# Graph attention with residual and layer norm on one core: third tile's masks ahead of the second table, x by rows a quad at a time, an early flag, set-up waits reordered

## The reference

```python
def _L0_gnn_ref(inlayer, adj_mat, W, w1, b1, w2, b2):
    in_fts = W @ inlayer.T
    f1 = (w1 @ in_fts).T + b1
    f2 = (w2 @ in_fts).T + b2
    logits = f1 + f2.T
    bias_mat = jnp.where(adj_mat > 0, 0.0, NEG_INF).astype(logits.dtype)
    coefs = jax.nn.softmax(jax.nn.leaky_relu(logits) + bias_mat, axis=-1)
    vals = coefs @ inlayer
    return vals
x = _layernorm(x + _L0_gnn_ref(x, adj, ...), axis=-1)
```

## Time and profile before

| what | us |
|---|---|
| time, median of 3 runs (273.82 to 276.17) | 274.12 |
| the profiled execution | 275.19 |
| its span, first to last instruction | 273.5 |
| PE busy | 258.2 |
| DVE busy | 242.6 |
| ACT busy | 195.6 |
| POOL busy | 67.2 |

### The profile page before, as it was taken

The page is one execution under the profiler, slowest core; times in us unless marked ns, Lnnn a source line. Parts: engine busy times, 40 slices in busy tenths (PEclk is TensorE's granted clock), DMA queues, the critical chain, the costliest instruction groups (busy, mean ns, idle before and its releaser), DMA issues.

```text
span 273.5 us, 5997 instructions
## 1 busy us (share of the span) xinstructions
PE 258.2 (94%) x2195; PEld 225.6 (82%) x2195; DVE 242.6 (89%) x309; ACT 195.6 (72%) x296; POOL 67.2 (25%) x98
## 2 busy tenths in 40 slices
PE   2999988799999999999999999999999999999991
PEld 2989877688888888888888888888888888888880
DVE  2888999988888899999999999999998999999963
ACT  2479999949999996999199919991999198003140
POOL 4002046930000006300630063006300630054150
PEclk9999999999999999999999999999999999999998
DMA  6999999999999999999999999999999999801011
GB/s 196 256 298 309 311 313 282 285 272 311 313 315 318 315 314 315 323 339 315 316 324 342 318 316 280 361 328 327 240 335 309 309 285 337 226 2 38 0 49 31
DMA packets 22562, 73.64 MB, mean 269 GB/s; under 512 B 3090, under 2 KB 4244, under 8 KB 22548
## 3 DMA queue, kind: packets, MB, share of 16 engines
q1 hardware_dynamic: 11184, 35.17, 42.9%
q10 hardware_dynamic: 9956, 34.64, 42.0%
q0 software_dynamic: 1408, 3.67, 4.7%
HBM read 71.37 MB, written 2.10 MB: 269 GB/s over the span
## 4 chain that ended last, share of the span: by engine, by line
DVE 58%; PE 16%; issue 8%; ACT 7%; DMA 7%; DVEq 1%; ACTq 1%; POOL 1%; POOLq 0%
DVE mn L743 19%; PE ps L1091 16%; DVE msk L756 11%; DVE mn L748 11%; DMA nat<-in_adj 5%; DVE post L855 3%; ACT sgn L474 3%; DVE ybt L870 2%; DVE bns L875 2%; ACT bt L542 2%; DVE ntot L860 2%; DVE post L857 2%; ACT post L518 2%; DMA msk<-in_x 2%; DVE mv L879 1%
## 5 line engine op out<-in xcount | busy, mean ns | idle before, releaser
L1091 PE MATMUL ps<-bt,msk 128*128 128x258 f16 x2048 | 232.1, 274 | 3.6 <-DVE msk L756 2.7
L1091 PEld LDWEIGHTS ps<-bt,msk 128*128 128x128 fp8e5 x2048 | 200.5, 98 | 34.2 <-issue 4.6
L474 ACT ACTIVATE sgn<-f2b,nf1l 128x1024 int8<-128x1024 f32 x128 | 136.4, 1144 | 5.2 <-POOL flag L409 4.0
L743 DVE TENSOR_SCALAR mn<-nat 128x4096 int8<-128x4096 int32 x32 | 73.1, 2284 | 5.0 <-DMA nat<-in_adj 4.6
L416 POOL TENSOR_SCALAR nmr<-mv 128x4 f32<-128x4 f32 x7 | 12.8, 1835 | 143.5 <-DVE mv L879 143.5
L756 DVE STREAM_TRANSPOSE msk<-mn 128x1024 uint32<-128x1024 uint32 x32 | 39.8, 1245 | 2.6
L748 DVE SCALAR_TENSOR_TENSOR mn<-sgn,mn 128x1024 uint32<-128x1024 uint32 x32 | 39.2, 1225 | 3.0 <-ACT sgn L474 2.0
L623 ACT ACTIVATE ybt<-ybt,nmr,rstd 128x128 f32<-128x128 f32 x28 | 11.5, 483 | 38.7 <-POOL nmr L421 38.7
L616 ACT ACTIVATE post<-ps,ac 128x258 f32<-128x258 f32 x60 | 24.8, 467 | 10.9 <-PE ps L1091 10.9
L761 DVE TENSOR_SCALAR msk<-msk 128x1024 uint32<-128x1024 uint32 x32 | 22.2, 695 | 1.0
L427 POOL DMA_DIRECT2D out<-ybt x24 | 13.7, 572 | 16.3 <-ACT ybt L623 14.9
(11 more groups left out here) (115 smaller groups left out, 105.2 us busy)
## 6 DMA issues: line engine op xcount, KB each, us to landing
nat<-in_adj SPq DMA_DIRECT2D x64, 512.0 KB, 15.1
nat<-in_adj ACTq DMA_DIRECT2D x64, 512.0 KB, 17.6
xn<-in_x POOLq DMA_DIRECT2D x4, 512.0 KB, 19.8
out<-ybt POOLq DMA_DIRECT2D x24, 64.0 KB, 6.6
msk<-in_x SPq DMA_DIRECT2D x8, 128.0 KB, 4.2
msk<-in_x ACTq DMA_DIRECT2D x8, 128.0 KB, 4.5
out<-ybt SPq DMA_DIRECT2D x4, 64.0 KB, 1.8
out<-post SPq DMA_DIRECT2D x4, 32.0 KB, 2.4
```

The costliest lines, as they stand in the source:

```text
L474: ins = act.activation(sgn[:, c, g * JA:(g + 1) * JA], f2b[:, :], ACT.Sign, bias=nf1l[:, bass.ds(G * t + g, 1)], scale=-1.0)
L743: dve.tensor_scalar(mn[:, c % 2], nat[:, c], 0, EDGE, ALU.is_gt, ALU.mult).then_inc(cast_done, 1)
L1091: ins = pe.matmul(ps[:, 2 * c + m, 0:2 * DV], mask_f[c][m][:, n // KB, n % KB, :], btv[m][:, n, :], start=(n == 0), stop=(n == NK - 1))
```

## The change

It does the following, and nothing else:

- **DVE, tile 2.** `cast`, `combine` and `turn` of tile 2 now stand in the middle of table 0's work, right behind the first chunk's `scale_x`. Table 0's chunks are made in the order 1, 0, 2, 3 (`ORDER`), ACT scales chunk 0 alone (`scale_act`), DVE the other three. ACT's `signs` of tile 2 stand ahead of all of table 0's `split_x`, and those of tile 3 have two `split_x` in between.
- **PE.** The minus sums of tile 2 stand ahead of all plus sums, and the plus sums of tiles 0, 1 and 2 are interleaved by chunk. In tile 0's minus sums all four `gram` stand behind the first chunk.
- **Table 1.** DVE scales chunk 3 for its larger part, and ACT only four blocks instead of eight. All `scale_x` stand ahead of the first cast, and `low_x` of chunks 2 and 3 behind the second `spread_f1`.
- **x by rows.** `xn` comes a quad at a time: quads 0 and 1 (eight transfers of 64 KB) where the four transfers of 512 KB were, and each later quad in POOL's loop ahead of a store. The loop is written out instead of being a loop in registers.
- **Flag.** Three of POOL's range tests stand ahead of the loads of `xn`, and the rest are four instructions instead of ten.
- **Set-up.** Only one block's f2 comes from PE, and two blocks' from ACT by sums. The bias product b1 + b2 comes ahead of `f1_columns`; the first `spread_f1` stands behind the fourth product of f2 on DVE, ahead of its sum; the copy of the first `nf1l` is ACT's and stands ahead of `xT_out(2)`; `xT_out(4)` and `xT_out(5)` come later than the fifth and sixth did, among `signs` and `split_x`.

```diff
@@ POOL @@
+            def load_rows(q, s):
+                for g in range(G):
+                    pool.dma_start(xn[g * SQ:(g + 1) * SQ, QT * q:QT * (q + 1), :],
+                                   x_g[g][:, QT * q:QT * (q + 1)]).then_inc(xn_in[s], 16)
+            pool.wait_ge(gst_ready, 1)
+            pool.tensor_tensor(rng[:, 0:1], gst[:, 0:1], gst[:, 1:2], ALU.add).then_inc(rng_step, 1)
...
             pool.wait_ge(f1_made, 2)
             pool.wait_ge(cast_done, 2)
-            for g in range(G):
-                pool.dma_start(xn[g * SQ:(g + 1) * SQ, :, :], x_g[g]).then_inc(xn_in, 16)
+            load_rows(0, 0)
+            load_rows(1, 1)
...
-                with pool.Fori(1, NQ // 2) as turn:
+                for turn in range(1, NQ // 2):
+                    load_rows(2 * turn, 0)
                     store(2 * turn - 2, 0)
                     rows(2 * turn - 1, 1)
+                    load_rows(2 * turn + 1, 1)
                     store(2 * turn - 1, 1)
                     rows(2 * turn, 0)
@@ ACT @@
             xT_out(1)
-            load_far(1, 1)
-            xT_out(2)
...
+            act.wait_ge(nf1_made, 1)
+            act.activation(nf1l[:, 0:FIRST * KB], ps[:, 6, 384:384 + FIRST * KB], ACT.Copy).then_inc(nf1l_ready, 1)
+            xT_out(2)
...
-            xT_out(4)
-            signs(0, 0, between=lambda: xT_out(5))
+            signs(0, 0, between={1: lambda: xT_out(4)})
             load_far(3, 3)
             split_x(1, 0)
-            xT_out(6)
+            xT_out(5)
+            split_x(1, 1)
...
             rows_out()
+            act.wait_ge(nf1l_ready, 2)
+            signs(2, 2)
+            act.wait_ge(cast_done, 2)
+            load_far(QT + 1, 1)
+            split_x(0, 1)
             scale_act(0)
             split_x(0, 0)
...
-            signs(3, 3, between=next_tile)
+            signs(3, 3, between={1: lambda: split_x(0, 2), 2: lambda: split_x(0, 3)})
@@ DVE @@
             dve.wait_ge(cs_ready[0], 1)
+            scale_x(0, 1)
+            stat_max(1, 2, 4)
+            cast(2, 2, 0)
+            stat_out(1, 2, 4)
+            combine(2, 2)
+            dve.wait_ge(y_ready[0], 1)
+            turn(2, 2)
+            plus(0, 0)
+            low_x(0, 1)
+            plus(1, 1)
             scale_x(0, 2)
-            stat_max(1, 2, 4)
+            low_x(0, 0)
             scale_x(0, 3)
-            plus(0, 0)
-            low_x(0, 0)
-            plus(1, 1)
-            stat_out(1, 2, 4)
-            low_x(0, 1)
+            dve.wait_ge(y_act, 1)
+            plus(2, 2)
             low_x(0, 2)
             low_x(0, 3)
-            cast(2, 2, 0)
-            combine(2, 2)
-            dve.wait_ge(y_act, 2)
-            turn(2, 2)
-            plus(2, 2)
             cast(3, 3, 0)
@@ PE @@
-            for h in range(BCH):
-                plus_sums(h, range(2))
             pe.wait_ge(xT_ready, NB)
             pe.wait_ge(turn_done, 3)
             edge_sums(2, 1)
-            for h in range(BCH):
-                plus_sums(h, [2])
+            pe.wait_ge(den_ready[0], 1)
+            pe.wait_ge(xeps_ready, 1)
+            plus_sums(ORDER[0], range(2))
+            plus_sums(ORDER[1], range(2))
+            plus_sums(ORDER[0], [2])
+            plus_sums(ORDER[1], [2])
+            plus_sums(ORDER[2], range(3))
+            plus_sums(ORDER[3], range(3))
```

More of the change, by code:

```diff
@@ L447, in _ @@
             with pool.Else():
+                for q in range(2, NQ):
+                    load_rows(q, q % 2)
                 with pool.Fori(0, NT) as t:
@@ L469, in load_far, with signs @@
                     load_part(act, t, c, a)
-            def signs(t, c, between=None):
+            def signs(t, c, between={}):
                 for g in range(G):
@@ L520, in scale_act, with scale_first @@
                 ins.then_inc(y_act, 1)
+            def scale_first():
+                act.wait_ge(cs_ready[1], 1)
+                for i in range(KB):
+                    n = (BCH - 1) * CN + i
+                    ins = act.activation(ybuf[:, BCH - 1, i], xl_chunk(BCH - 1)[:, i], ACT.Copy, scale=cs[:, 1, n:n + 1])
+                ins.then_inc(y1_act, 1)
             def rows_out():
@@ L801, in _ @@
             turn(0, 0)
-            scale_x(1, 2)
             low_x(1, 1)
-            low_x(1, 2)
             spread_f1(1, FIRST * KB, NK, 7, 0)
@@ L977, in _ @@
                 dve.wait_ge(g_f2_ready, 2 * A)
-                dve.wait_ge(xn_in, 16 * G)
+                for i in range(2):
+                    dve.wait_ge(xn_in[i], 8 * G * NQ)
                 STEPS = 7
@@ L1154, in _ @@
             edge_sums(3, 1)
-            for h in range(BCH):
+            for h in ORDER:
                 plus_sums(h, [3])
```

200 lines of the change are left out of this document (93 added, 107 removed).

## The result

| what | before | changed |
|---|---|---|
| median of twelve runs, us | 274.64 | 276.52 |
| lowest to highest | 273.59 to 276.52 | 275.80 to 278.08 |
| the profiled execution | 275.19 | 275.80 |
| its span | 273.5 | 273.6 |
| time outside the span, median | 1.7 | 2.1 |

The ratio of the times is 1.0074, with a 95% interval of 1.0052 to 1.0097. The changed kernel is 2 us slower. I had forecast 273.5 and a range up to 275.8. By the bound of 1% this is the case to which I gave 0.82, but the sign was wrong, and the range too short by 0.7 us. Of the 3.0 us between forecast and median, 0.5 is the base: I had started from the median of three runs of the kernel before, 274.12, and twelve give 274.64.

What follows compares the result with a forecast made beforehand. PE was taken to bound the kernel: time before tile 2, 215 us of products, 6.1 us of tail. The 0.6 us gain ahead of tile 4 gave 274.6 like the profiled run, median 273.5, range 271.8 to 275.8.

Steps and rivals of the forecast that it cites:

- the case to which I gave 0.82: Whole kernel: time the same within 1% (2.7 us), between 271.4 and 276.9 us; chance 0.82.
- What bounds the kernel: Whole kernel: time before tile 2, plus PE's unbroken 215 us of products, plus 6.1 us behind the last.
- my 51 to 54: POOL's flag: ready at 51 to 54 us, DVE wants it at 58.6; its coming earlier is worth 0.
- The written-out loop on POOL: 0 ... The tail is unchanged.: POOL's loop and the end: writing the loop out costs 0, as POOL mostly waits; the tail stays as it was.
- Cost on the path 0: x by rows, a quad at a time in the loop: costs 0; without tile 10's cover at most 0.9 us per quad.
- The new waits: PE's set-up: 1.1 us of waiting for `xT_out(2)`, and 0 to 0.5 for `xT_out(5)`.
- the gain of 0.6 us: PE up to tile 4's first product: 66.1 us instead of 66.75, the whole gain of the change.
- the 44 that I had named as a sign of being wrong: PE's unbroken row: prediction wrong if it starts before 44 us with DVE ready earlier than forecast.
- my 44.6: PE at tile 2: minus sums can start at 44.6 us (30.5 plus DVE's 14.1), against 52.42.
- DVE was the bound after all: Rival: DVE bounds the kernel, relief from 4.6 us of waits for `adj` counts with the 0.6; 269 us, chance 0.07.
- The clock falls: Rival: PE's clock drops in 2.4 us of idle ahead of tile 2, costing 1.6 us; 275.1 us, chance 0.08.
- POOL is held up at its loads: Rival: POOL's x issues cost over about 1.7 us each, flag late; at 3 us each 283 us, chance 0.03.

Runs made afterwards that it cites:

- e2: The kernel before with POOL's loop over quads written out and nothing else; 274.23 us, ratio 0.9992.
- e5: The kernel before with 28 more loads of 512 bytes each on POOL's queue, loop still in registers; 276.11 us, ratio 1.0036.
- e6: The changed kernel with a drain in each of POOL's three turns; 276.15 us, ratio 1.0035.
- e12: The changed kernel with x by rows in one go (4 issues of 512 KB) and drains in POOL's turns; 274.30 us, ratio 0.9968.
- e16: e6 with 14 products nobody uses ahead of PE's wait for tile 2's masks; 275.34 us, ratio 1.0025.
- e9: The changed kernel with each load of x for quads 2 to 7 bringing 2 KB instead of 64 KB, still 58 issues; 276.72 us, ratio 1.0060.
- e3: The kernel before with x by rows a quad at a time on POOL's queue and the loop written out; 276.83 us, ratio 1.0084.
- e1: The changed kernel with x by rows again in four transfers of 512 KB on POOL's queue; 274.70 us, ratio 1.0029.
- e13: e9 with 14 products nobody uses ahead of PE's wait for tile 2's masks; 276.30 us, ratio 1.0063.
- e14: The changed kernel with 14 products nobody uses ahead of PE's wait for tile 2's masks; 276.21 us, ratio 1.0071.
- e7: The changed kernel with drains in POOL's turns and the last quad's stores issued a tile at a time; 275.12 us, ratio 1.0028.
- e8: The kernel before with drains in POOL's turns and the last quad's stores issued a tile at a time; 274.60 us, ratio 0.9987.
- e11: The kernel before with x by rows in three parts, drains in POOL's turns and the loop written out; 275.91 us, ratio 1.0043.
- e10: The changed kernel with x by rows in three parts (38 issues) and drains in POOL's turns; 275.15 us, ratio 1.0007.
- e15: e12 with POOL's loop in registers and 14 products nobody uses ahead of PE's wait for tile 2's masks; 274.80 us, ratio 1.0015.
- e4: The changed kernel with x by rows (32 transfers of 64 KB) on SP's queue and POOL's loop in registers; 296.75 us, ratio 1.0819.

## Why the prediction was wrong

**What bounds the kernel: right up to the last product.** PE never waited behind tile 2, DVE's waits for `adj` and ACT's for the flag were hidden from PE, and the flag brought nothing. POOL had it ready at 55.9, later than my 51 to 54, and DVE came to it at 57.8. What failed is the step from PE's end to the program's. I had read "6.1 us behind the last product" as DVE's chain behind PE. It was two chains, and POOL's drain ended within half a microsecond of SP's, out of sight of all rows I had quoted.

**"The written-out loop on POOL: 0 ... The tail is unchanged."** This is the first step that failed: the tail was 7.9 us instead of 6.1. I had priced each new issue by its time on POOL (0.81 us, hidden) and by its bytes (hidden), not by what it leaves for the end. The written-out loop is innocent (e2); the 28 issues in it aren't: by themselves they make 2.3 us of drain, and 1.0 us of time by the ratio or 1.5 by the medians (e5).

**x by rows: "Cost on the path 0".** This is the second. For PE it held in the profiled execution. But DVE's position at the end counts too, and the 2.14 us that it had in hand stood in the earlier trace rows, which I used for another purpose. In the changed kernel's timeline a tile costs DVE 5.54 us (from the cast at 241.85 to the next at 247.39) and a quad's moments 5.6 (from 252.96): 27.8 us of the 28.7 that PE takes for a quad. So DVE gains at most 0.9 us a quad on PE, and it gains that in the kernel before as well, where it is just as full (27.9 us from the cast at 158.28 to the one at 186.17). What it loses against the kernel before by a wait, 1.4 us at 146 us and 0.2 for tile 29 at 230.6, it doesn't get back by the end: it came out 1.4 us later against PE. Nor did its waits for `adj` shrink, as I had forecast: 4.8 us instead of 4.6. By e6 and e12, which have the short drain, this costs up to 1.85 us; by e16 it is 0.5 to 1.0.

**The sum of the two.** The end is the later of two chains, and each of my two steps lengthens one of them. In us behind the last product, from the traces:

| kernel | DVE's idle time ahead of the last join | SP at its drain | POOL's drain ends | span ends |
|---|---|---|---|---|
| before | 2.14 | 5.8 | 5.4 | 6.1 |
| e5 (issues alone) | 2.33 | 5.9 | 7.7 | 7.9 |
| e6 (x in the loop, short drain) | 0.24 | 6.6 | 2.9 | 6.9 |
| changed | 0.70 | 6.9 | 7.6 | 7.9 |
| e9 (issues, little of x) | 2.78 | 5.8 | 7.6 | 7.9 |
| e3 | none | 7.9 | 8.7 | 8.9 |
| e12 (neither) | 2.77 | 5.8 | 2.9 | 6.1 |

In the changed kernel's trace POOL's drain alone sets the tail, and DVE's lateness costs nothing beside it: with DVE in time (e9) the tail is the same. With the drain short (e6) the lateness is what is left, 0.8 us of tail. Where DVE has no time in hand at all (e3), POOL's chain is late as well, and both count. In executions without a profile the shares are not known. By the medians e5 and e6 cost 1.5 us each and the two together 1.9 to 2.2 (changed, e3); by the ratios it is 1.0 each and 2.0 to 2.3, so the times alone don't show whether the two add.

**Outside the span** I had counted no change, and it is 0.4 us. It seems to go with the transfers written down in POOL's program rather than with those that run: 1.7 in the kernel before and in e5 (58 run, most of them in a loop), 1.8 in e1, e2 and e12, 2.0 in e3, 2.1 in the changed kernel, e9, e13 and e14. That isn't shown: in e6, e7 and e16, which have the same transfers and the drains, single executions have either 1.8 to 1.9 or 2.2 to 2.4 us.

**From the start to tile 2: the steps came as forecast, but the gain didn't.** The new waits were 0.84 and 0.48 us (I had 1.1, and 0 to 0.5). DVE's chain from the second `spread_f1` (29.50) to PE's start on tile 2 (43.62) took 14.1 us, as summed, and PE's idle time was 1.6 to 2.3 (2.4). But the first mask product came later against the first work on x than I had it. Before, 22.9 us lie between them (29.30 - 6.38, and the same in e2, e3 and e5; 23.3 and 23.5 in e8 and e11); in the twelve traces with the new set-up it is 24.0 (changed, e10, e14, e16) to 25.5 (e7). On the mean the loss is 1.5 us instead of 1.1 (24.53 less 23.08). Of the gain of 0.6 us nothing can be seen at the end of PE's row: from the first work on x to the last product it is 260.4 to 261.1 us (mean 260.8) in five traces with the old set-up and unbroken rows, and 260.3 to 261.9 (mean 261.0) in eight with the new, e9 with its lower clock apart. So the 0.6 us of my sum is the third term that failed. That the profiled execution ended its products 1.6 us earlier than the one before is for 1.05 us an earlier arrival of x (PE's first row at 5.33 against 6.38), before any step that the change moves. For the same reason the row on tile 2 started at 43.62, ahead of the 44 that I had named as a sign of being wrong: counted from the first work on x it came within 0.1 us of my 44.6.

**The rivals.** *DVE was the bound after all* had the right engine and the wrong sign: I let it count in the loop only, as a gain. *The clock falls* is a real case, seen once in the eight traces with the new order and 1.6 to 2.3 us of idle time there, worth 1.56 us (I had 1.6). It isn't the cause (e14). *POOL is held up at its loads* occurs as well. In the changed kernel the line of x's loads reads

```profile
L377 POOL DMA_DIRECT2D xn<-in_x x32: 551/554/2541, 35.0 to 250.3; - x32
```

and the first load of POOL's first turn started at 105.84, beside DVE's cast from 105.76 on (2.29 us), and took 2.33. The hold-up is 2 us, which POOL's idle time hides. The rule of the Trainium skill that I had set aside (SBUF — State Buffer, A bandwidth-pool intuition that's wrong) is about this; the trace agrees in kind with 2.5 us for the longest issue.

**Still open** are how the 1.5 to 2 us are shared out between the two causes in executions without a profile, what the 0.4 us outside the span come from, and what the new order by itself is worth with x in one go: e1, e12 and e15 lie from 0.5 us under to 0.1 above the kernel before, about the width of their intervals. I took e1's long runs for x in one go beside an earlier tile 10, but e12 and e15, which load it alike, show hardly any, so that isn't shown.

## What to carry to other kernels

Follow each engine to its last instruction, the drain included, before calling a tail unchanged, and note how far behind the last chain the next one ends. Transfers on GpSimd's queue have a price per issue that is paid at the end of the program, so few large ones are better there, and a drain while GpSimd is idle pays for them early. And where two engines are almost equally full, look at how much time the second has in hand at the very end: it is a budget, and a transfer that makes the loop's own loads late is taken from it.

## What the runs showed of the hardware

- POOL's drain at the end of the program took about 0.5 us plus 0.08 us for each transfer issued from its queue, whatever was moved: 2.66 us at 26, 2.97 at 30, 5.25 at 58, and 0.5 where a drain in the loop had come ahead of it. The same count doesn't give the drains in the loop (4.7 to 12.2 us in e6). The Trainium skill (VectorE: DVE Perf Modes, The DRAIN you can't avoid) tells of short drains of constant length that the runtime's code adds on all engines. The drains read here stand at this program's own end (L68): ACT's is as short as those (8 ns), and POOL's isn't.
- A transfer of 64 KB in rows of 512 bytes was 32 packets from POOL's queue and 144 from SP's. From SP's it took, by estimate from the pages of e4 and the changed kernel, 7.6 to 12.6 us a MB of the DMA engines' time, from POOL's 3.7, and `adj` 3.4.
- Behind the issue of the last store SP came to its drain after 2.4 us where that store was 128 rows (64 KB; e7, e8), and after 1.6 to 1.9 where it was 32 rows (16 KB).
- PE's granted clock after it stood still: at the lower level after 2.25 us once (e9) and at the full one after 2.26 and 2.28 (e7, e10); in e4's trace at the full one after 1.37, 2.18 and 2.31, at the lower one after 2.72, 3.03 and 5.05, each time for 16 to 21 products at twice the distance.
